# Attention stage of a graph layer with routed experts: raw rows turned and projected, variance by ScalarE's accumulator, five buffers of x

## What is computed

```python
x = x + gnn(layernorm(x), ...)          # 100000 edges, softmax over each node's edges, 8 heads of 32
# and then the experts on a = layernorm(x), 8 of them, 2 for each node:
logits = a @ Wr + br
top_p, top_idx = top_k(softmax(logits), 2)
xn = layernorm(a)
h = gelu((xn * ln_g[e] + ln_b[e]) @ W1[e] + b1[e]);  y = h @ W2[e] + b2[e]
x = x + weighted sum of the two experts' y
```

## Time and profile before

| | |
|---|---|
| median of the runs | 2183.68 us (2181.82 to 2191.77, 3 runs) |
| span of the profiled execution | 2179.1 us, mean granted TensorE clock 0.967 |
| busy, share of the span | PE 94%, PEld 74%, DVE 71%, ACT 59%, POOL 59% |
| `attend`, first to last instruction of VectorE | 1221.1 to 1306.0 us, 3.9% of the span |

### The profile page before, as it was taken

The page is one execution under the profiler, slowest core; times in us unless marked ns, Lnnn a source line. Parts: engine busy times, 40 slices in busy tenths (PEclk is TensorE's granted clock), DMA queues, the critical chain, the costliest instruction groups (busy, mean ns, idle before and its releaser), DMA issues. The chain is left out here.

```text
span 2179.1 us, 40886 instructions
## 1 busy us (share of the span) xinstructions
PE 2044.9 (94%) x11567; PEld 1610.2 (74%) x11568; DVE 1545.8 (71%) x3782; ACT 1277.0 (59%) x3507; POOL 1279.5 (59%) x1434
## 2 busy tenths in 40 slices
PE   7799999999999999999999585999999999999997
PEld 5566667666666666666766485998888888888886
DVE  8589999999999999999998878344333334344332
ACT  4688888878888887877887465332222333322222
POOL 2377777777777777777777000455555555555554
PEclk9899999999999999999999757999999999999998
DMA  8766555655655555565564967122222222222221
GB/s 258 218 184 178 171 176 174 179 171 169 182 172 174 178 176 173 169 180 170 171 181 133 323 226 132 39 34 34 36 34 36 34 34 34 34 34 35 35 36 24
DMA packets 164043, 279.58 MB, mean 128 GB/s; under 512 B 36736, under 2 KB 115361, under 8 KB 163778
## 3 DMA queue, kind: packets, MB, share of 16 engines
q0 software_dynamic: 66720, 149.75, 28.9%
q1 hardware_dynamic: 88618, 121.01, 17.5%
q10 hardware_dynamic: 8568, 7.25, 1.0%
HBM read 240.94 MB, written 36.97 MB: 128 GB/s over the span
## 5 line engine op out<-in xcount | busy, mean ns | idle before, releaser
L647 POOL DMA_INDIRECT arena<-h_tab,src x880 | 845.0, 960 | 312.0 <-issue 242.2
L1611 ACT ACTIVATE arena<-psum,arena 128x128 f32<-128x128 f32 x840 | 239.4, 368 | 558.1 <-PE psum L1551 558.1
L813 PE MATMUL psum<-arena 128*128 128x256 f32 x1760 | 478.8, 395 | 1.2 <-issue 1.2
L834 PE MATMUL psum<-arena 128*128 128x264 f32 x1760 | 475.7, 394 | 0.7 <-DVE arena L925 0.7
L1551 PEld LDWEIGHTS psum<-arena 128*128 128x128 f32 x3360 | 386.2, 193 | 44.3 <-DVE arena L1634 25.3
L1551 PE MATMUL psum<-arena 128*128 128x128 f32 x3360 | 404.1, 279 | 8.4 <-DVE arena L1634 6.5
L834 PEld LDWEIGHTS psum<-arena 128*128 128x128 f32 x1760 | 321.9, 191 | 96.1 <-issue 45.4
L1585 PE MATMUL psum<-arena 128*128 x1680 | 384.3, 382 | 0.6
L813 PEld LDWEIGHTS psum<-arena 128*128 128x128 f32 x1760 | 318.4, 191 | 81.9 <-issue 37.0
L1585 PEld LDWEIGHTS psum<-arena 128*128 128x128 f32 x1680 | 311.3, 190 | 45.6 <-issue 5.0
L905 DVE SCALAR_TENSOR_TENSOR arena<-arena,a_dst,psum 128x512 f32<-128x512 f32 x440 | 325.5, 740 | 14.0 <-ACT arena L713 6.3
(11 more groups left out here) (225 smaller groups left out, 1939.4 us busy)
## 6 DMA issues: line engine op xcount, KB each, us to landing
arena<-rel_list SPq DMA_DIRECT2D x110, 512.0 KB
arena<-in_W SPq DMA_DIRECT2D x16, 1024.0 KB, 12.5
arena<-h_tab,src POOLq DMA_INDIRECT x880
arena<-ea_slots SPq DMA_DIRECT2D x440, 27.0 KB
arena<-in_x SPq DMA_DIRECT2D x12, 896.0 KB, 8.8
h_tab<-arena SPq DMA_DIRECT2D x6, 924.0 KB, 6.6
out_rows<-arena SPq DMA_DIRECT2D x5, 896.0 KB, 5.0
xn<-arena ACTq DMA_DIRECT2D x5, 896.0 KB, 6.7
```

The costliest lines, as they stand in the source:

```text
L647: pool.indirect_dma_start(rows[:, s % RING, k, :], None, d.h_tab[:, :], bass.IndirectOffsetOnAxis(ap=c.src[:, s * U + k:s * U + k + 1], ax ...
L813: last = nc.tensor.matmul(ps[:, HDT + x, y * UE:(y + 1) * UE], hj[:, (s // 2 * 2 + y) % HJ, x * P:(x + 1) * P], oht[:, half % OT, (u + y) ...
L834: last = nc.tensor.matmul(ps[:, AGG + a % 2, 0:HS], oh[:, a % OH, k, :], rows[:, a % RING, k, :], start=(k == 0), stop=(k == U - 1))
L1611: last = nc.scalar.activation(hT[:, b, h * P:(h + 1) * P], ps[:, UP + 2 * b + n, h % 4 * P:(h % 4 + 1) * P], ACT.Gelu, bias=b1_now[:, b, h ...
```

## The change

TensorE now turns the raw rows of the new x and not the normalised ones. The router's weights are first centred (each column minus its mean, made with two multiplies by a matrix of ones, the weights and VectorE) and get a ninth column of ones. So one projection gives the product with centred rows and the row's sum. VectorE takes these nine sums per tile out of PSUM, one group at a time (`take_sums`), and makes minus the mean of each row. ScalarE makes the variance: a Square of each tile with minus the mean as bias, its accumulator's sum written to PSUM. `bn_stats` and `merge_stats` go, and so do ScalarE's copies of the turned tiles, which VectorE now makes (`take_xT`). There are five PSUM banks of turned tiles for three, `project` follows `turn` by four tiles and not two, and the new x has five buffers for three. Groups 3 and 4 of x are loaded at the start of `attend`; all eight experts' `W2` are loaded in `route`.

```diff
-W2_LATE = 6
-XB = 3
+W2_LATE = X
+XB = 5
+X_EARLY = 3
 XB_AT = W2_AT
 XB_END = W2_AT + W2_LATE * (HID // P) * IN
 XT_AT = ACC_AT + 2 * KH * HID + 2 * HID
...
@@ -692,7 +693,7 @@
 
             sp.wait_ge(hd_done, SLOTS)
             sp.wait_ge(alpha_made, 2 * NCH)
-            for b in range(XB):
+            for b in range(X_EARLY):
                 sp.dma_start(c.x2[b][:, 0:TILES[b], :], d.x[FIRST[b] * P:FIRST[b + 1] * P, :].rearrange("(k p) i -> p k i", p=P)).then_inc(c.x_loaded[b], 16)
             w1 = c.arena[:, W1_AT:W1_AT + W1_WORDS].rearrange("p (k e n) -> p k e n", k=KH, e=X)
             for e in range(X):
...
             return c.arena[:, at - n:at]
 
+        XTB = (0, 1, 2, 5, 6)
+        SUMS, VAR = (3, 4), 7
+        COLS = X + 1
...
+        SQUARES = 3
+        square = take(SQUARES * IN).rearrange("p (b i) -> p b i", b=SQUARES)
         ps = c.psum
-        LG = 3
         LAST = len(TILES)
-        bank = lambda n: n % 3
+        bank = lambda n: n % len(XTB)
+        place = [(i, k) for i in range(LAST) for k in range(TILES[i])]
...
         @block.sync
         def _(sp):
             def load(i):
+                if i >= XB:
+                    sp.wait_ge(x2_stored[i % XB], 16 * (i // XB))
+                    sp.wait_ge(xn_made, FIRST[i - XB + 1])
                 sp.dma_start(rows_of(i), d.x[group(i), :].rearrange("(k p) i -> p k i", p=P)).then_inc(x_loaded[i % XB], 16)
 
-            for e in range(W2_LATE, X):
-                sp.dma_start(c.w2[:, e], d.W2[e].rearrange("(h p) n -> p h n", p=P)).then_inc(c.w2_loaded, 16)
+            for i in range(X_EARLY, XB):
+                load(i)
             for i in range(LAST):
                 sp.wait_ge(x2_made, i + 1)
                 sp.dma_start(d.out[group(i), :].rearrange("(k p) i -> p k i", p=P), rows_of(i)).then_inc(x2_stored[i % XB], 16)
-                if i and i - 1 + XB < LAST:
-                    sp.wait_ge(x2_stored[(i - 1) % XB], 16 * ((i - 1) // XB + 1))
-                    sp.wait_ge(xn_made, FIRST[i])
-                    load(i - 1 + XB)
+                if XB <= i + 2 < LAST:
+                    load(i + 2)
...
         @block.scalar
         def _(act):
             def deviations(i):
-                act.wait_ge(var_made, i + 1)
-                var = mv[:, 3, 0:TILES[i]]
+
+                act.wait_ge(taken, 2 * i + 2)
+                if i == 0:
+                    act.wait_ge(weights_made, KH + 1)
+                for k in range(TILES[i]):
+                    n = FIRST[i] + k
+                    if n >= SQUARES:
+                        act.wait_ge(squared, n - SQUARES + 1)
+                    nc.scalar.activation(square[:, n % SQUARES, :], x2[i % XB][:, k, :], ACT.Square, bias=minus_mean[:, n:n + 1],
+                                         accum_out=ps[:, VAR, n:n + 1]).then_inc(squared, 1)
+                act.wait_ge(squared, FIRST[i + 1])
+                var = ps[:, VAR, tiles_of(i)]
                 nc.scalar.activation(sd[:, 0, tiles_of(i)], var, ACT.Sqrt, bias=c.eps[:, :], scale=1.0 / IN)
                 nc.scalar.activation(sd[:, 1, tiles_of(i)], var, ACT.Sqrt, bias=eps2, scale=(1.0 + LN_EPS) / IN).then_inc(sd_made, 1)
 
...
-            deviations(0)
-            for i in range(LAST):
+            def normalise(i):
+
                 act.wait_ge(scale_made, 2 * (i + 1))
                 if i >= 2:
                     act.wait_ge(xn_stored[i % 2], 16 * (i // 2))
                 for k in range(TILES[i]):
-                    normalise(i, k)
-                    if k >= 2:
-                        take_xT(FIRST[i] + k - 2)
-                    if k == min(TILES[i], GT - 1) - 1 and i + 1 < LAST:
-                        deviations(i + 1)
+                    n = FIRST[i] + k
+                    nc.scalar.activation(xn[:, i % 2, k, :], x2[i % XB][:, k, :], ACT.Identity, bias=shift[:, n:n + 1], scale=rs[:, n:n + 1]).then_inc(xn_made, 1)
                 act.wait_ge(xn_made, FIRST[i + 1])
                 act.dma_start(d.xn[group(i), :].rearrange("(k p) n -> p k n", p=P), xn[:, i % 2, 0:TILES[i], :]).then_inc(xn_stored[i % 2], 16)
...
+            for i in range(LAST):
+                deviations(i)
+                if i:
+                    normalise(i - 1)
+            normalise(LAST - 1)
...
         @block.tensor
         def _(pe):
-            place = [(i, k) for i in range(LAST) for k in range(TILES[i])]
-
             def turn(n):
                 i, k = place[n]
-                pe.wait_ge(xn_made, n + 1)
-                if n >= 3:
-                    pe.wait_ge(xT_copied, n - 2)
+                pe.wait_ge(x2_made, i + 1)
+                if n >= len(XTB):
+                    pe.wait_ge(xT_copied, n - len(XTB) + 1)
                 for m in range(KH):
-                    last = nc.tensor.transpose(ps[:, bank(n), m * P:(m + 1) * P], xn[:, i % 2, k, m * P:(m + 1) * P], c.ident[:, :])
+                    last = nc.tensor.transpose(ps[:, XTB[bank(n)], m * P:(m + 1) * P], x2[i % XB][:, k, m * P:(m + 1) * P], c.ident[:, :])
                 last.then_inc(xT_made, 1)
 
             def project(n):
+                i, k = place[n]
                 pe.wait_ge(xT_copied, n + 1)
+                if i >= 2:
+                    pe.wait_ge(taken, 2 * i - 2)
+                if n == 0:
+                    pe.wait_ge(weights_made, KH + 1)
                 for m in range(KH):
-                    last = nc.tensor.matmul(ps[:, LG, n * X:(n + 1) * X], xT[:, bank(n), m * P:(m + 1) * P], c.wr[:, m, :],
+                    last = nc.tensor.matmul(ps[:, SUMS[i % 2], k * COLS:(k + 1) * COLS], xT[:, bank(n), m * P:(m + 1) * P], weights[:, m, :],
                                             start=(m == 0), stop=(m == KH - 1))
-                last.then_inc(logits_made, 1)
-
+                last.then_inc(projected, 1)
+
+            for m in range(KH):
+                last = nc.tensor.matmul(ps[:, VAR, 0:X], c.ones[:, :], c.wr[:, m, :], start=(m == 0), stop=(m == KH - 1))
+            last.then_inc(weights_summed, 1)
+            BEHIND = 4
             for n in range(J):
                 turn(n)
-                if n >= 2:
-                    project(n - 2)
-            project(J - 2)
-            project(J - 1)
+                if n >= BEHIND:
+                    project(n - BEHIND)
+            for n in range(J - BEHIND, J):
+                project(n)
 
         @block.vector
         def _(dve):
             sums = acc.rearrange("p (k n) -> p k n", n=HS)
 
+            def centre_weights():
+
+                nc.vector.memset(weights[:, :, X:COLS], 1.0).then_inc(weights_made, 1)
+                dve.wait_ge(weights_summed, 1)
+                for m in range(KH):
+                    nc.vector.scalar_tensor_tensor(weights[:, m, 0:X], ps[:, VAR, 0:X], -1.0 / IN, c.wr[:, m, :], ALU.mult, ALU.add).then_inc(weights_made, 1)
...
@@ -1197,50 +1221,62 @@
                 dve.wait_ge(mean_made, i + 1)
                 dve.wait_ge(biased, i + 1)
                 nc.vector.tensor_tensor(rows_of(i), rows_of(i), att[:, 0:TILES[i] * IN].rearrange("p (k i) -> p k i", k=TILES[i]), ALU.add).then_inc(x2_made, 1)
-                dve.wait_ge(x2_made, i + 1)
-                for k in range(TILES[i]):
-                    nc.vector.bn_stats(st[:, k, :], x2[i % XB][:, k, :]).then_inc(stats, 1)
-                dve.wait_ge(stats, FIRST[i + 1])
-                if i:
-                    dve.wait_ge(sd_made, i)
-                merge_stats(nc, dve, st[:, 0:TILES[i], :], mv[:, :, 0:TILES[i]], i, merged, var_made)
+
+            def take_xT(i, k0, k1):
+
+                for k in range(k0, k1):
+                    n = FIRST[i] + k
+                    dve.wait_ge(xT_made, n + 1)
+                    if n >= len(XTB):
+                        dve.wait_ge(projected, n - len(XTB) + 1)
+                    nc.vector.tensor_copy(xT[:, bank(n), :], ps[:, XTB[bank(n)], 0:IN]).then_inc(xT_copied, 1)
+
+            def take_sums(i):
+
+                dve.wait_ge(projected, FIRST[i + 1])
+                nc.vector.tensor_copy(sums_of[:, tiles_of(i), :], ps[:, SUMS[i % 2], 0:TILES[i] * COLS].rearrange("p (k n) -> p k n", n=COLS)).then_inc(taken, 1)
+                dve.wait_ge(taken, 2 * i + 1)
+                nc.vector.tensor_scalar(minus_mean[:, tiles_of(i)], sums_of[:, tiles_of(i), X], -1.0 / IN, None, ALU.mult).then_inc(taken, 1)
...
             nc.vector.memset(eps2, LN_EPS * LN_EPS)
             add_bias(0)
             shares(0, 0, FIRST[2])
             mean_of_rows(0)
             add_rows(0)
+            centre_weights()
             add_bias(1)
-            scales(0)
             mean_of_rows(1)
+            take_xT(0, 0, TILES[0])
             add_rows(1)
             shares(1, FIRST[2], J)
-            scales(1)
-            add_bias(2)
-            mean_of_rows(2)
-            for i in range(2, LAST):
-                add_rows(i)
+            take_sums(0)
+            for i in range(1, LAST):
+                n = TILES[i]
```

(42 more changed lines are left out.)

23 lines of the change are left out of this document (5 added, 18 removed).

## The result

The changed kernel takes 2213.07 us (median of 4 runs, 2211.49 to 2214.18) where the kernel before took 2183.32 beside it (4 runs, 2181.82 to 2191.77): a ratio of 1.0129, 95% interval 1.0105 to 1.0154 (the quotient of the two medians alone is 1.0136). It is slower by some 30 us; 2219 was predicted, 2205 to 2228 the range. The profiled span is 2209.6 us (before: 2179.1).

A forecast was written before the change was run, and what follows sets the result against it. It took full VectorE to bound `attend`, then its waits for TensorE: 34.7 us of standstills, 2.1 less own work and a ScalarE tail of 17.7 made the stage 35.2 us longer, so 2183.7 + 35.2 = 2219 us; range 2205 to 2228.

The forecast's parts named there:

- What bounds the stage: In `attend`, 85.4 us long, VectorE is full at 19.80 of 20 us; TensorE is nearly full at 18.30.
- The standstill: At `take_sums`, VectorE waits for four turns and four projections on TensorE: 4.88 us for a full group, 34.7 together.
- Rival B: In `attend`, same wait at `take_sums` with TensorE at full clock: pair 0.67 us, wait 2.9, kernel 2205; chance 0.10.
- A: In `attend`, the wait at `take_sums` with TensorE at its low clock, 1.17 us a pair: 2213 to 2227; chance 0.82.
- Rival C: At `take_sums`, the four pairs are done when VectorE gets there, so the kernel is not slower: 2184; chance 0.05.
- VectorE's own work: In `attend`, VectorE drops 22.1 us of work and takes on 20.0, gaining 2.1; between 4.5 gained and 2.5 lost.
- The period: In `attend`, one iteration of a group of seven tiles takes 13.8 us where it took 9.23.
- ScalarE's tail: At the end of `attend`, after `take_sums(7)`, ScalarE finishes two groups one after the other and stores: 17.7 us.
- What was costed at nothing: Loads of x in `attend`, and `W2`, `b1` and gates loads in `route`: nothing, at most 2 us if gates land late.
- The sum: Whole kernel: `attend` ends at 1341.2 for 1306.0, 35.2 us more; 2183.7 + 35.2 = 2219 us.

The follow-up runs named there:

- the first experiment: Changed kernel with only TensorE's order altered: all projections of a group come before the next group's first turn; 2184.21 us, ratio 1.0021 to the kernel before.
- the second: Changed kernel with only VectorE's order altered: `take_sums(i)` comes behind `add_bias(i+2)` and the scales move one iteration on; 2202.91 us, one run.
- fourth: Changed kernel with half of each projection left out, only the first of a tile's two halves multiplied; 2198.72 us, one run.
- the fifth experiment: Changed kernel with two extra multiplies of 128x512 on TensorE ahead of each group's first turn, their result unused; 2204.84 us, one run.
- the kernel with both orders: Changed kernel with a group's projections ahead of the next group's turns and `take_sums(i)` behind `add_bias(i+2)`; 2182.74 us, ratio 1.0004 to the kernel before.

## Why the prediction held, step by step

*What bounds the stage.* Right. The stage grew by 117.0 - 85.4 = 31.6 us, and the trace has VectorE waiting 35.6 us at the place named, released by the projection.

*The standstill.* 4.88 each was said for groups 1 to 6, then 4.5, 0.9, together 34.7. Measured: 4.96 six times, 4.64 and 0.93, and a small one of 0.32 ahead of the last sums, which the sum had left out: 6 x 4.96 + 4.64 + 0.93 + 0.32 = 35.6. The 1.17 us a pair of the earlier trace rows went over unchanged, and 0.28 in place of 0.2 is what the wait has beyond four pairs. That the cause is order is shown by the first experiment (5.0 us of wait left), its size by the second and fourth, where it moved by one `add_bias` and by four half projections. The price was right because the clock stayed low; at the pace of the full clock the same order costs 2.8 a group, as the fifth experiment shows.

*Rival B, the clock.* The granted clock is 0.50 in both windows above, as the earlier trace rows had it, so A and not B. The Trainium skill, TensorE: Matmul & The Clock Gate, Part 1, has work lift TensorE to its full clock. In the kernel with both orders TensorE was busy 20.00 of 20 us at 0.50, and with the extra multiplies it was busy 7.49 of 10 at 0.84. The measurement decides: a high busy share in this profile does not mean the full clock. What in these transposes and narrow multiplies keeps it low stays open.

*Rival C.* Where the four pairs are done when VectorE comes to the sums, as in the kernel with both orders, the time is within 0.1% of before, 2182.74, near the 2184 it was priced at. It decides where it was put, at `take_sums`.

*VectorE's own work.* Copies came one every 0.333 us: three in 1.08 and four in 1.41, as the earlier trace rows said. The Trainium skill, VectorE: DVE Perf Modes, section on the TRN2 errata, would have them at an estimated 0.39 each; one alone does last 0.42 here, but in a run each adds only 0.333. Without all its waits the stage is 85.4 - 12.7 = 72.7 us for VectorE before (7.0, 5.1 and 0.6 of waits) and 117.0 - 47.7 = 69.3 after (35.6, 7.0, 5.1), so it gained 3.4 where 2.1 was said, in the bounds. The period, 13.8, was measured at 13.81 to 13.82, and the last sums but one ended 101.7 us into the stage (1320.70) where 102.4 was said.

*ScalarE's tail* is the mis-sized term: 17.7 us said, 1335.5 - 1320.7 = 14.8 measured. Its timeline, against the earlier trace rows:

```profile
1327.06 0.51 ACT L1129 ACTIVATE arena<-arena 128x256 f32<-128x256 f32 x1 [0.50 <-ACT arena L1143]
1327.47 0.15 ACT L1129 ACTIVATION_READ_ACCUMULATOR arena<-arena 128x1 f32 x1
1327.53 0.49 ACT L1129 ACTIVATE arena<-arena 128x256 f32<-128x256 f32 x1
...
1328.57 0.26 ACT L1133 ACTIVATE arena<-psum,eps 128x3 f32<-128x3 f32 x1
1328.73 0.26 ACT L1134 ACTIVATE arena<-psum,arena 128x3 f32<-128x3 f32 x1
1328.88 2.06 ACT L1143 ACTIVATE arena<-arena 128x256 f32<-128x256 f32 x4
```

The accumulator is a second small instruction, as was supposed, but it lies almost wholly beside the next Square: a tile takes 0.44 to 0.47 us (0.47 from 1327.06 to 1327.53), not 0.51, and the roots some 0.5 to 0.6 with their wait, not 0.7. So `deviations(8)` is 1.8 for 2.3 and `deviations(7)` 2.3 for 2.8. The larger part is the last store: issued at 1333.05, it landed 2.5 us later where the 4.3 of the earlier trace rows was taken. The same store of 384 KB took 4.3 us in the kernel before and 2.5 in the changed kernel and in all eight of the experiments; why, no run here tells. The normalisations were as said.

*What was costed at nothing.* Right in each case. The loads of x never made VectorE wait. SyncE issued `b1` between 17.9 and 20.8 us into `route` and the gates at 1359.13, 23.1 into it, as before; they landed 18.6 us later, and `route` lasted 52.1 us for 53.2.

*The sum.* Of the 5.9 us between 2219 and 2213.07 the tail makes 2.9, the way to it 0.7, the start of the stage at 1219.02 for 1221.09 another 2.1; `route` is 1.1 shorter and `experts` 2.1 longer (821.5 for 819.4), and the median lies 3.5 us above the profiled span for 4.6. (The changed kernel's profiled run, 2211.49, was only 1.9 above its span; the rest is that it was faster than the median.) The start of the stage lay between 1217.1 and 1225.0 in kernels whose code up to there is the same, so 2 us of it is no effect of the change. The stage itself grew by 31.6 us for the 35.2 of the prediction, and 2213.07 lies at the lower edge of the range of 2213 to 2227 that it gave to A alone: the mechanism held as told, and the tail was priced too high.

## What to carry to other kernels

When two engines' orders are written by hand, look at each wait for what stands ahead of its releaser in the other queue: a software pipeline that runs four tiles deep across a group's border put four tiles of the next group between VectorE and its sums, and both engines fell to between 58 and 74% busy in their windows. Price such a loop by the chain through both queues, not by either engine's busy time, and repair the order before counting buffers: the standstill gave each load room that the mended order takes away. Where the loop is mended and still nothing is gained, read the end of the stage: here these were waits for ScalarE's roots, its last normalisations and its stores, and handing seven normalisations to VectorE gave 1 us of the stage and nothing that the kernel's time shows.

## What the runs showed of the hardware

An ACTIVATE with an accumulator brings a second instruction of its own, ACTIVATION_READ_ACCUMULATOR, 0.15 to 0.19 us long, which starts 0.1 us before the ACTIVATE ends. One Square started every 0.45, about 0.04 more than the 0.41 that the prediction estimated without it; the same Square without an accumulator was not run. A square root that reads its operand from PSUM took 0.26 to 0.27 us where one from the arena took 0.29 to 0.30. TensorE's granted clock, in one stage and with the same mix, was 0.67, 0.84 and 0.50 in three neighbouring windows once two wide multiplies a group were added (0.50 is the level of 1.2 GHz, the other two are means of both levels), and the stage with more work on TensorE was the shorter one, 109.9 us for 117.0.
